# Message loop of a graph network: 9 semaphore updates of TensorE a group in place of 36, and 16 gathers a group without waits for count reads

## The reference

```python
h = relu(layernorm(x))                                   # 12500 x 32
m = concat([h[src], edge_attr], axis=1)                  # 200000 x 48
m = relu(m @ w1a + b1a) @ w1b + b1b                      # 48 -> 96 -> 96
agg = segment_sum(m, dst) / max(count(dst), 1)
x = x + relu(concat([h, agg]) @ w2a + b2a) @ w2b + b2b
feat0 = f = relu(layernorm(x))
for _ in range(10):                                      # propagation
    f = f * src_norm
    f = 0.9 * segment_sum(f[src], dst) * dst_norm + 0.1 * feat0
x = x + f
```

## Time and profile before

| | before |
|---|---|
| median of three executions | 6986.83 us |
| span of the profiled execution | 7018.8 us |
| the profiled execution's own time | not listed apart from its span |
| message loop, first gather of the loop to its last | 248.9 to 2696.7 us |
| last seven groups, without gathers | 2698 to 2791 us |
| TensorE busy | 5576.3 us, 79% of the span |
| VectorE busy | 4279.1 us, 61% |
| GpSimd busy | 1693.3 us, 24% |
| ScalarE busy | 721.3 us, 10% |
| TensorE's mean granted clock | 0.880 |

### The profile page before, as it was taken

One profiled execution on the slowest core, in us unless ns is written; L12 is line 12 of the kernel. 1 busy time (PEld: TensorE's weight loads), 2 busy tenths in 40 slices (PEclk: granted clock), 3 DMA queues, 4 the chain that ended last, 5 costly groups with the idle time before them and its releaser, 6 DMA issues. The chain is left out here.

```text
span 7018.8 us, 211605 instructions
## 1 busy us (share of the span) xinstructions
PE 5576.3 (79%) x85008; PEld 3590.0 (51%) x85008; DVE 4279.1 (61%) x12668; ACT 721.3 (10%) x1695; POOL 1693.3 (24%) x1739
## 2 busy tenths in 40 slices
PE   1455555555555556589999999999999999999998
PEld 1344444444444445446565554656555565656564
DVE  7455555555555557766666666666656666666665
ACT  0122222222222223000000000000000000000000
POOL 5655555555555552500000000000000000000000
PEclk9867676666667767799999999999999999999999
DMA  4322222222222222155545555555555555555554
GB/s 117 77 75 76 76 76 77 75 76 77 79 72 79 72 76 94 27 205 194 200 183 204 192 198 205 189 200 191 201 191 201 191 201 201 189 203 189 197 197 169
DMA packets 442864, 1016.61 MB, mean 145 GB/s; under 512 B 253162, under 2 KB 371914, under 8 KB 387354
## 3 DMA queue, kind: packets, MB, share of 16 engines
q1 hardware_dynamic: 386938, 968.76, 39.0%
q0 software_dynamic: 54944, 33.96, 2.6%
HBM read 838.78 MB, written 176.58 MB: 145 GB/s over the span
## 5 line engine op out<-in xcount | busy, mean ns | idle before, releaser
L1864 PE MATMUL banks_fast<-count_units_fast,feature_parts_fast 128*32 128x512 fp8e3 x70608 | 3826.3, 379 | 31.6 <-DVE count_units_fast L1759 26.9
L1864 PEld LDWEIGHTS banks_fast<-count_units_fast,feature_parts_fast 128*32 128x32 bf16 x70608 | 2146.2, 97 | 1688.5 <-issue 37.5
L1758 DVE TENSOR_SCALAR count_units_fast<-packed_ring_fast 128x512 int32<-128x512 int32 x2949 | 1255.8, 426 | 1429.1 <-PE banks_fast L1864 1398.2
L144 POOL DMA_INDIRECT rows_fast<-row_table,idx_fast x1456 | 1408.5, 967 | 996.9 <-ACT count_stage_fast L1257 563.4
L1759 DVE TENSOR_SCALAR count_units_fast<-packed_ring_fast 128x512 int32<-128x512 int32 x2949 | 1237.2, 420 | 0.0
L1351 PE MATMUL banks_fast<-w1a_b1a_fast,turn_fast 49*128 49x96 f32 x3136 | 374.6, 375 | 810.6 <-ACT turn_fast L1262 589.6
L1223 DVE TENSOR_SCALAR window_place_hot_fast<-iota_wide_fast,local_keys_fast,target_weight_fast 128x196 bf16<-128x196 f16 x3136 | 933.9, 343 | 0.0
L1316 PE MATMUL banks_fast<-window_place_hot_fast,window_src_hot_fast 128*128 128x196 bf16 x3136 | 697.4, 312 | 115.4 <-issue 71.0
L1322 PE MATMUL banks_fast<-window_place_hot_fast,window_src_hot_fast 128*128 128x196 bf16 x3136 | 680.2, 305 | 106.1 <-issue 105.4
L1351 PEld LDWEIGHTS banks_fast<-w1a_b1a_fast,turn_fast 49*128 49x128 f32 x3136 | 294.9, 260 | 917.4 <-issue 497.4
L1316 PEld LDWEIGHTS banks_fast<-window_place_hot_fast,window_src_hot_fast 128*128 128x128 bf16 x3136 | 410.1, 155 | 224.2 <-issue 148.3
(11 more groups left out here) (282 smaller groups left out, 1551.5 us busy)
## 6 DMA issues: line engine op xcount, KB each, us to landing
packed_ring_fast<-edge_counts SPq DMA_DIRECT2D x422, 1792.0 KB, 7.0
edge_counts<-count_stage_fast SPq DMA_DIRECT2D x100, 784.0 KB
running_sums<-run_sums_fast SPq DMA_DIRECT2D x100, 768.0 KB
rows_fast<-row_table,idx_fast POOLq DMA_INDIRECT x1456
rows_fast<-attrs_padded SPq DMA_DIRECT2D x98, 128.0 KB
attrs_padded<-in_edge_attr SPq DMA_DIRECT2D x1, 12500.0 KB
rows_fast<-row_table,src_ends_fast POOLq DMA_INDIRECT x112
row_table<-h_nodes_fast SPq DMA_DIRECT2D x1, 1568.0 KB, 5.2
```

The costliest lines, as they stand in the source:

```text
L144: pool.indirect_dma_start(out=self.rows[:, r, c, 0:DN], out_offset=None, in_=b.dram.table, in_offset=bass.IndirectOffsetOnAxis(ap=idx[:, c ...
L1758: nc.vector.tensor_scalar(to[..., 0:P // 8], of, NIBBLES, None, ALU.bitwise_and)
L1864: last = nc.tensor.matmul(b.banks[at:at + DN, SWEEP[m % 2], 0:COLS], parts[:, side, j, k * DN:(k + 1) * DN], of_strip.bitcast(FP8), start= ...
```

## The change

TensorE's updates in a group are cut to nine. `turned` is raised by `turn_rows(0)` alone. `mixed` is raised by `turn_rows(1)`, `turn_rows(2)`, `turn_rows(3)` and the last matmul of `mix(3)`; since TensorE works in order, each stands for the mix before it too. `counted` is raised once a quarter, behind its four rows, and `hot_used` is gone. `keys_turned` is raised once, ahead of the loop. Those who wait are changed to match: the relu of quarter q waits for the event that follows its mix, ScalarE waits for counts once a quarter, VectorE waits for `counted` before it writes a mask buffer again, and GpSimd and SyncE wait for `turn_rows(3)` under its new name. GpSimd issues the 16 gathers of its step one after the other.

```diff
 GpSimd
-                pool.wait_ge(turned, (SLOTS + g + 1) * Q)
+                pool.wait_ge(mixed, (SLOTS + g + 1) * Q - 1)
...
-                for u in range(READS):
-                    if u:
-                        pool.wait_ge(count_read, (SLOTS + g + 1) * READS - READS // Q + u)
-                        pool.sem_inc(taken, 1)
-                    ahead.gather(pool, b, r, idx[:, r, :], range(u * G // READS, (u + 1) * G // READS))
+                ahead.gather(pool, b, r, idx[:, r, :], range(G))
 SyncE
-                    sp.wait_ge(turned, (g + 1) * Q)
+                    sp.wait_ge(mixed, (g + 1) * Q - 1)
 VectorE
+            dve.wait_ge(keys_turned, 1)
...
-                        dve.wait_ge(keys_turned, k + 1)
...
-                        dve.wait_ge(hot_used, g * (WG // 2) + (q + 1) * (QW // 2))
+                        dve.wait_ge(counted, g * Q + (q + 1))
 ScalarE
-                        act.wait_ge(counted, g * READS + (u + 1))
-                        act.sem_inc(passed, 1)
+                        if u % (READS // Q) == 0:
+                            act.wait_ge(counted, g * Q + (u // (READS // Q) + 1 + SLOTS))
+                            act.sem_inc(passed, 1)
...
-                        act.wait_ge(turned, SLOTS * Q + g * Q + (q + 1))
+                        if q == 0:
+                            act.wait_ge(turned, g + 1)
...
-                        act.wait_ge(mixed, 2 * g * Q + 2 * (q + 1))
+                        act.wait_ge(mixed, (SLOTS + g) * Q + (q + 1))
 TensorE
-            pe.sem_inc(hot_used, SLOTS * (QW // 2))
+            pe.sem_inc(counted, SLOTS)
...
-                last.then_inc(keys_turned, 1)
+                return last
...
-            turn_keys(0)
-            pe.sem_inc(turned, SLOTS * Q)
+            turn_keys(0).then_inc(keys_turned, 1)
+            pe.sem_inc(mixed, SLOTS * Q)
...
-                        if side:
-                            last.then_inc(counted, 1)
...
-                        last.then_inc(hot_used, 1)
+                        if (r + 1) % (QW // 2) == 0:
+                            last.then_inc(counted, 1)
...
-                        last.then_inc(turned, 1)
+                        last.then_inc(mixed if q else turned, 1)
...
-                            if k >= QC - 2:
-                                last.then_inc(mixed, 1)
+                        if q == Q - 1:
+                            last.then_inc(mixed, 1)
```

More of the change, by code:

```diff
@@ L1038, in messages_and_counts @@
         first_act = sb("first_act", [P, 1])
-        hot, hot_used, counted, count_read, local_made, filled, keys_pointed, keys_turned, tailed, all_summed = (
-            sem("window_hot"), sem("window_hot_used"), sem("window_counted"), sem("counts_read"), sem("keys_local"), sem("loop_filled"),
+        hot, counted, count_read, local_made, filled, keys_pointed, keys_turned, tailed, all_summed = (
+            sem("window_hot"), sem("quarter_counted"), sem("counts_read"), sem("keys_local"), sem("loop_filled"),
             sem("keys_pointed"), sem("keys_turned"), sem("tail_kept"), sem("all_summed"))
```

## The result

The changed kernel takes 7385.85 us, median of 4 executions (7382.45 to 7397.93), against 6983.73 for the kernel before in the same comparison: a ratio of 1.0577 [1.0564, 1.059], 402 us slower. The profiled execution took 7385.01 us, its span is 7383.5.

What follows compares the result with a forecast made beforehand. Each group was taken as bound by its gathers' drain plus one bare handoff and restart: 23.8 + 0.44 + 0.76 + 1.44 + 0.99 = 27.4 us against 26.9, +45 us over 91 groups, about 7031 us; range 6760 to 7270.

Steps and rivals of the forecast that it cites:

- The wait w: Delay of a TensorE update to ScalarE during GpSimd's gathers in the message loop; taken as 6.6 us each.
- handoff: TensorE's transposes releasing ScalarE's copy or relu, then the next mix; one was forecast bare after the drain.
- the drain: Gathers occupying something TensorE's updates also need, about 1.44 us each, 23.8 us a group; late updates arrive at its end.
- The row behind the 6.6: In the old loop a mix ended at 2200.36 us and its relu started at 2206.92; this supplied w.
- sticking rival: Message loop: w above 7.0 us puts a second handoff behind the drain; 29.6 us a group, about 7230 us; chance 0.23.
- the case in which none does: Message loop: no update passes during the drain, so a third handoff follows it; 31.6 us a group, about 7415 us.
- quarter 0's transposes end 5.8 us after the restart: Start of TensorE's group cycle: four count rows, mix, four more and transposes put the first update 5.8 us after GpSimd restarts.
- The other row, 8.8 us: Second evidence for w, from the early gathers without pauses: VectorE took up TensorE's finished buffer 8.8 us later.
- The price of sticking: After the drain, the second bare handoff was charged another 0.76 + 1.44 us, giving 29.6 us a group, +245 us.
- The edits counted at nothing: Changed waits on VectorE, SyncE and GpSimd, later count reads and later relus were counted at no cost of their own.
- The streaks of 16 or 17 with one pause a group: Sign of being right: GpSimd issues 16 or 17 gathers, then pauses once a group until TensorE's transposes release it.

Runs made afterwards that it cites:

- 1.48 us: Changed kernel with a 256-column iota (GpSimd filling an unread tile) behind each gather, slowing issue to 1.48 us; ratio 0.9785 to the kernel before.
- all36_unpaced: Kernel before with all 36 updates a group, only GpSimd's pauses for count reads taken away; ratio 1.0577 to the kernel before.
- without pauses: Pair with 16 gathers in a row: kernel before without its pauses (36 updates) and changed kernel (nine); both 1.0577 to the kernel before.
- the old pauses: Pair with seven waits for count reads: kernel before (36 updates), and changed kernel with those waits put back (nine), ratio 0.9976.
- the iota: Pair with a 256-column iota on GpSimd behind each gather: changed kernel (nine updates) 0.9785, kernel before without pauses (36) 0.9939.
- one gate: Pair with one mid-group GpSimd wait for TensorE's second transposes: changed kernel (nine updates) 1.0131, kernel before with it replacing seven waits (36) 1.0073.
- 64-column iotas: Changed kernel with a 64-column iota on GpSimd behind each gather, issuing one in 1.32 us; ratio 1.0617 to the kernel before.
- three gathers under way: Changed kernel with each gather waiting until the one three earlier in its group has landed; ratio 1.0391 to the kernel before.
- 1.50 us a DMA: Changed kernel with a 288-column iota on GpSimd behind each gather; ratio 0.9804 to the kernel before.
- 1.53 us: Changed kernel with a 320-column iota on GpSimd behind each gather; ratio 0.9764 to the kernel before.

## Why the prediction was wrong

**The wait w: the step that failed.** The prediction took one w of 6.6 us for each handoff, so that the second would be in at 20.8 us and only the third arrive with the drain. In the changed kernel the first handoff takes 7.0 us on average, close to 6.6, but the second stands until the drain of the streak, 11.0 us on average and 14.6 us in the first group shown. So two handoffs, and not one, fall behind the drain. The row behind the 6.6 measured a wait that the drain of eight gathers had ended, 11 us into a streak; for a handoff that stands until the drain of sixteen it was a lower bound. The two average 9.0 us: by the prediction's own condition (w above 7.0 us) this is its sticking rival, which it gave 0.23. The first handoff passes in all 90 groups, so it isn't the case in which none does. That one's 7415 us lies nearer to the result than the sticking one's 7230 by chance, since the price of sticking was too low; by its own terms (0.37 + 1.44 on top of 29.6) it would be 31.4 us a group, and not 31.6.

The sum also had quarter 0's transposes end 5.8 us after the restart. They end at 2.7 us at the median. Its 2.54 us for four count rows come from a stretch with a granted clock of 0.50 (1.2 of 2.4 GHz, 2196.77 to 2199.31 us); the group shown has 1.00 from 2226.0 to 2230.2 us. With 2.7 in place of 5.8 and w at 6.6 the third handoff would still have ended behind the drain, so this changed no case.

**The other row, 8.8 us,** was read as coming from the nearest streak without pauses. These are GpSimd's first and last gather of that stretch in the kernel before:

```profile
49.14 2.02 POOL L144 DMA_INDIRECT rows_fast<-row_table,src_ends_fast  x1 [6.31 <-DVE feature_parts_fast L490]
...
119.16 1.59 POOL L144 DMA_INDIRECT rows_fast<-row_table,src_ends_fast  x1 [0.30 <-issue]
```

48 gathers, 47 steps in 70.02 us, are one in 1.49 us on average, with stretches at 1.25 between slower ones. Handoffs at 1.48 us take up to 8.7 us and don't stand until the streak's end, and neither did these. So the row says little of sixteen gathers at 1.25 us: besides the missing pause, the pace had to match.

**The price of sticking was too low.** The rival said 29.6 us, the group takes 30.92. After the drain it had two handoffs of 0.76 + 1.44 and 0.44 for count reads, with the restart 5.83 us; the trace shows 7.95. The second mix can't follow its copy: the copy ends at 2253.76, and the mix starts at 2255.51, behind quarter 1's four count rows, which stand ahead of it in TensorE's fixed order (1.75 us). TensorE has been idle for 12.8 us before, and the first mix and transposes take 1.79 us in place of 1.44, at a granted clock of 0.50 (2251.1 to 2253.0 us; 0.72 in the stretch that gave 1.44); the restart takes 1.43 in place of 0.99, and no count reads stand in the way (-0.44). With the drain this group, which has no key fetch, is 22.65 + 7.95 = 30.60 us. The count rows' part is read from the timeline; no run took them away.

**What held.** The drain, 1.41 to 1.47 us a gather, is 1.42 at the median. The edits counted at nothing cost nothing that shows in the sum: all36_unpaced, which has none of them, ends like the change; what they cost, the fewer updates gave back. The streaks of 16 or 17 with one pause a group came as described.

**Updates.** The Trainium skill ("TensorE: Matmul & The Clock Gate", "The cost: per-tile semaphore tail") gives 26.3 ns for an update; 27 fewer are by that an estimate of 27 x 26.3 ns = 0.71 us a group. The runs agree in none of four pairs. They differ with what else is in the way: nothing without pauses; 0.19 us with the old pauses, by the medians (6984.35 - 6967.14 over 91; the 0.45 of the traces comes from a profiled execution before that was slow for its kernel); 1.38 us with the iota; and 0.48 us lost with one gate. What sets an update's price here isn't shown.

## What to carry to other kernels

When a wait has no releaser in the profile and ends in a burst, ask what was issued at the same time, and compare the issue pace with the pace at which the bursts end: here 1.25 against 1.41 us. An engine slowed a little can be worth more than one that never waits; try its pace as a parameter before removing its waits. Sum the handoffs of a group before and after, since the mean of the waits that the profile lists can fall while their number grows. And a measured wait that something else ended is a lower bound only.

## What the runs showed of the hardware

While GpSimd issues indirect DMAs of 128 rows one in 1.25 us, TensorE's semaphore updates reach ScalarE and VectorE late. The first handoff of a group, its transposes done 2.7 us into the streak at the median, took 7.0 us on average. The second, done 12.3 us into it at the median, stood until 1.42 us a DMA from the streak's start (22.65 us with 16, 24.12 with 17); with 64-column iotas it was 1.43 in the streak shown, (2044.73 - 2020.45)/17. ScalarE's updates to TensorE passed in the same streaks within 0.33 us. At 1.48 and 1.50 us a DMA TensorE's handoffs took 3.1 and 3.2 us on average, at 1.53 us 0.8. The landing of the rows is not what they wait for: with three gathers under way, landing at 1.25 us, a relu still waited 11.7 us. Which part of the chip they share stays open; no run here names it.
